# A graph attention layer: ten of 32 row tiles get one product of 258 columns in place of two

## The reference

```python
h = maximum(layernorm(x), 0.0)
h = h @ W.T + b_W
e = (h @ a1)[:, None] + (h @ a2)[None, :] + b_a[0]
e = where(e > 0, e, 0.2 * e)
scores = where(adj > 0, e, -9e15)
out = x + softmax(scores, axis=1) @ h
```

## Time and profile before

| | |
|---|---|
| Median of 3 runs | 200.91 us (200.64 to 201.04) |
| The profiled execution | 200.99 us |
| Its span in the profile | 199.4 us |
| TensorE, products | busy 194.2 us (97%), 3183 instructions |
| TensorE, weight loads | busy 188.5 us (95%) |
| VectorE | busy 184.0 us (92%) |
| ScalarE | busy 142.7 us (72%) |
| GpSimd | busy 53.0 us (27%) |
| TensorE's granted clock | full (2.4 GHz) in all slices |
| Data moved | 75.66 MB, mean 379 GB/s |

### The profile page before, as it was taken

One profiled execution on the slowest core, in us unless ns is written; L12 is line 12 of the kernel. 1 busy time (PEld: TensorE's weight loads), 2 busy tenths in 40 slices (PEclk: granted clock), 3 DMA queues, 4 the chain that ended last, 5 costly groups with the idle time before them and its releaser, 6 DMA issues.

```text
span 199.4 us, 7226 instructions
## 1 busy us (share of the span) xinstructions
PE 194.2 (97%) x3183; PEld 188.5 (95%) x3183; DVE 184.0 (92%) x269; ACT 142.7 (72%) x164; POOL 53.0 (27%) x79
## 2 busy tenths in 40 slices
PE   7989999999999999999999999999999999999993
PEld 7758889999999999999999999999999999999992
DVE  4795987899999999999999999999999999999865
ACT  2598879988886888676888888858768888888100
POOL 1028999699999020430000000000000000000000
PEclk9999999999999999999999999999999999999999
DMA  5999999999999999999999999999999999999312
GB/s 172 371 417 415 368 406 421 421 426 412 423 417 420 417 417 421 414 419 424 416 414 422 419 421 422 416 422 417 417 411 416 412 396 421 421 413 293 98 39 69
DMA packets 16256, 75.66 MB, mean 379 GB/s; under 512 B 1632, under 2 KB 5984, under 8 KB 8032
## 3 DMA queue, kind: packets, MB, share of 16 engines
q1 hardware_dynamic: 16080, 75.06, 92.6%
q10 hardware_dynamic: 144, 0.13, 0.3%
HBM read 73.08 MB, written 2.11 MB: 377 GB/s over the span
## 4 chain that ended last, share of the span: by engine, by line
PE 95%; DVE 2%; ACT 1%; issue 1%; POOL 0%; POOLq 0%
PE ps L845 28%; PE ps L841 28%; PE ps L843 28%; PE ps L817 4%; PE ps L807 3%; PE ps L898 2%; ACT L401 1%; PE ps L829 1%; DVE den L492 1%; PE ps L924 1%; PE ps L831 0%; PE ps L853 0%; DVE xT L538 0%; DVE rg L496 0%; ACT hT L337 0%
## 5 line engine op out<-in xcount | busy, mean ns | idle before, releaser
L841 PE MATMUL ps<-V,w 128*128 128x130 f16 x1008 | 170.7, 220 | 0.0
L845 PE MATMUL ps<-V,w 128*128 128x130 f16 x1008 | 170.7, 220 | 0.0
L843 PE MATMUL ps<-V,w 128*128 128x128 f16 x1008 | 170.7, 219 | 0.0
L379 ACT ACTIVATE mask<-adj_sb 128x1024 bf16<-128x1024 int32 x126 | 126.3, 1049 | 33.1 <-DMA adj_sb<-in_adj_t 32.9
L446 DVE SCALAR_TENSOR_TENSOR w<-g_row,pairs,mask 128x1024 f32<-128x1024 f32 x96 | 119.4, 1298 | 1.0 <-ACT mask L379 0.9
L843 PEld LDWEIGHTS ps<-V,w 128*128 128x128 f16 x1008 | 98.6, 98 | 1.0 <-issue 1.0
L841 PEld LDWEIGHTS ps<-V,w 128*128 128x128 f16 x1008 | 98.6, 98 | 0.7 <-issue 0.7
L845 PEld LDWEIGHTS ps<-V,w 128*128 128x128 f16 x1008 | 98.7, 98 | 0.0
L446 DVE SCALAR_TENSOR_TENSOR w<-ps,pairs,mask 128x1024 f32<-128x1024 f32 x31 | 37.5, 1274 | 3.9 <-ACT mask L379 2.7
L797 POOL PARTITION_ALL_REDUCE bad<-bad x1 | 0.4, 382 | 110.6 <-DVE bad L519 110.6
L727 POOL TENSOR_TENSOR x_sb<-x_sb,b_row 128x512 f32<-128x512 f32 x8 | 10.9, 1404 | 0.0
(11 more groups left out here) (103 smaller groups left out, 67.0 us busy)
## 6 DMA issues: line engine op xcount, KB each, us to landing
adj_sb<-in_adj_t SPq DMA_DIRECT2D x64, 1024.0 KB, 10.4
xT<-in_x_t SPq DMA_DIRECT2D x8, 256.0 KB, 7.5
x_sb<-in_x_p SPq DMA_DIRECT2D x3, 512.0 KB, 12.0
g_row<-g_dram SPq DMA_DIRECT2D x3, 512.0 KB, 11.2
out<-xT SPq DMA_DIRECT2D x3, 512.0 KB, 9.6
x_sb<-in_x_p SPq DMA_DIRECT2D x2, 256.0 KB, 4.3
out<-xT SPq DMA_DIRECT2D x1, 192.0 KB, 3.2
out<-xT SPq DMA_DIRECT2D x3, 64.0 KB, 1.6
```

Of the source, the lines that this page charges most:

```text
L379: nc.scalar.activation(mask[:, m % MASKS, r], adj_sb[:, m % HELD, r], ACT.Relu, scale=CONNECTED).then_inc(mask_ready, 1)
L841: nc.tensor.matmul(sums[:, bank, a, :], w16[:, m % SLOTS, col:col + P, 1], V[:, jt, 0, 0:NF], start=(jt == 0 and a == 0), stop=False, skip ...
L843: nc.tensor.matmul(sums[:, bank, a, 0:DOUT], w16[:, m % SLOTS, col:col + P, 1], V[:, jt, 1, 0:DOUT], start=False, stop=False, skip_group_c ...
L845: return nc.tensor.matmul(sums[:, bank, a, :], w16[:, m % SLOTS, col:col + P, 0], V[:, jt, 0, 0:NF], start=False, stop=(jt == NT - 1), ski ...
```

## The change

V's layout becomes 128 columns of low V, then 128 of high V, then the two of e^v, 258 columns without a gap. Ten row tiles are "parted": one of the eight in groups 0 and 2 (k = 6), five in group 1 (k = 0 to 4), three in group 3 (k = 0, 2, 4). For these the two products of the high weight become one of 258 columns, which leaves high weight by low V in 128 columns of PSUM and all the rest in the 130 columns after them. The product of the low weight stays as it is, and adds into the 130. In the rows, VectorE takes both halves: one instruction for the low half, later one for the high half, which waits for the first over a new semaphore (rows_begun). The sums of weights are read at other places; in groups 0 and 2 this takes three reductions in place of two. PIECES becomes 2, 2, 2, 1, 1 row tiles (before 3, 2, 1, 1, 1). Before the first pair of group 1 TensorE gets one more wait, for the weights of all of group 0.

```diff
-    VW = DOUT + 8
+    HI = DOUT
+    VW = HI + NF + 6
+    MERGED = HI + NF
...
-    PIECES = ((0, 3), (3, 5), (5, 6), (6, 7), (7, 8))
+    PIECES = ((0, 2), (2, 4), (4, 6), (6, 7), (7, 8))
...
+        if group % 2 == 0:
+            return (k // 3, k % 3 * NF) if k < 6 else (2, (k - 6) * MERGED)
         if group < NG - 1:
-            return 3 * (group % 2) + k // 3, k % 3
-        return ((3, 0), (3, 1), (3, 2), (4, 0), (4, 1), (5, 0), (6, 0), (7, 0))[k]
+            return (3 + k, 0) if k < 5 else (k - 2, MERGED)
+        return ((3, 0), (3, MERGED), (4, 0), (4, MERGED), (5, 0), (5, MERGED), (6, 0), (7, 0))[k]
+    def parted(group, k):
+        if group % 2 == 0:
+            return k == 6
+        return k < 5 if group < NG - 1 else k in (0, 2, 4)
...
-        V = sb("V", [P, NT, 2, VW], F16)
+        V = sb("V", [P, NT, VW], F16)
...
+                def add_rows(group, k0, k1):
+                    for k in range(k0, k1):
+                        g = GI * group + k
+                        if parted(group, k):
+                            ins = nc.vector.scalar_tensor_tensor(Z[:, g, :], low_sums(group, k), rg[:, g:g + 1], x_sb[:, g, :],
+                                                                 ALU.mult, ALU.add)
+                            ins.then_inc(rows_begun, 1)
+                        else:
+                            ins = nc.vector.scalar_tensor_tensor(Z[:, g, :], high_sums(group, k)[:, 0:DOUT], rg[:, g:g + 1],
+                                                                 x_sb[:, g, :], ALU.mult, ALU.add)
+                    for k in range(k0, k1):
+                        g = GI * group + k
+                        if parted(group, k):
+                            dve.wait_ge(rows_begun, apart.index(g) + 1)
+                            ins = nc.vector.scalar_tensor_tensor(Z[:, g, :], high_sums(group, k)[:, 0:DOUT], rg[:, g:g + 1],
+                                                                 Z[:, g, :], ALU.mult, ALU.add)
+                    return ins
...
-                    nc.tensor.matmul(sums[:, bank, a, :], w16[:, m % SLOTS, col:col + P, 1], V[:, jt, 0, 0:NF],
-                                     start=(jt == 0 and a == 0), stop=False, skip_group_check=True)
-                    nc.tensor.matmul(sums[:, bank, a, 0:DOUT], w16[:, m % SLOTS, col:col + P, 1], V[:, jt, 1, 0:DOUT],
-                                     start=False, stop=False, skip_group_check=True)
-                    return nc.tensor.matmul(sums[:, bank, a, :], w16[:, m % SLOTS, col:col + P, 0], V[:, jt, 0, 0:NF],
+                    first = jt == 0 and sums_at(group, k)[1] == 0
+                    if parted(group, k):
+                        nc.tensor.matmul(both_sums(group, k), w16[:, m % SLOTS, col:col + P, 1], V[:, jt, 0:MERGED],
+                                         start=first, stop=(jt == NT - 1), skip_group_check=True)
+                    else:
+                        nc.tensor.matmul(high_sums(group, k), w16[:, m % SLOTS, col:col + P, 1], V[:, jt, HI:HI + NF],
+                                         start=first, stop=False, skip_group_check=True)
+                        nc.tensor.matmul(low_sums(group, k), w16[:, m % SLOTS, col:col + P, 1], V[:, jt, 0:DOUT],
+                                         start=False, stop=False, skip_group_check=True)
+                    return nc.tensor.matmul(high_sums(group, k), w16[:, m % SLOTS, col:col + P, 0], V[:, jt, HI:HI + NF],
                                             start=False, stop=(jt == NT - 1), skip_group_check=True)
...
                     if m == PAIRS:
                         pe.wait_ge(h_ready, NCH)
+                        pe.wait_ge(w_ready, 2 * PAIRS)
```

More of the change, by code:

```diff
@@ L96, in sums_at @@
     def sums_at(group, k):
+        if group % 2 == 0:
+            return (k // 3, k % 3 * NF) if k < 6 else (2, (k - 6) * MERGED)
         if group < NG - 1:
-            return 3 * (group % 2) + k // 3, k % 3
-        return ((3, 0), (3, 1), (3, 2), (4, 0), (4, 1), (5, 0), (6, 0), (7, 0))[k]
+            return (3 + k, 0) if k < 5 else (k - 2, MERGED)
[4 more added lines that the diff above has]
+        return k < 5 if group < NG - 1 else k in (0, 2, 4)
+    apart = [GI * group + k for group in range(NG) for k in range(GI) if parted(group, k)]
     with ExitStack() as ctx:
@@ L163, in gat_layer_kernel, with high_sums, low_sums, both_sums @@
         Z = xT[:].rearrange("p (g d) -> p g d", d=DIN)
-        sums = ps[:, :, 0:3 * NF].rearrange("p b (a n) -> p b a n", a=3)
+        def high_sums(group, k):
+            bank, at = sums_at(group, k)
+            at += HI if parted(group, k) else 0
+            return ps[:, bank, at:at + NF]
+        def low_sums(group, k):
+            bank, at = sums_at(group, k)
+            return ps[:, bank, at:at + DOUT]
+        def both_sums(group, k):
+            bank, at = sums_at(group, k)
+            return ps[:, bank, at:at + MERGED]
         w16 = w[:, :, :].rearrange("p a n -> p (a n)").bitcast(F16).rearrange("p (a n h) -> p a n h", a=SLOTS, h=2)
@@ L228, in gat_layer_kernel @@
         rg_ready = sem("rg_ready")
+        rows_begun = sem("rows_begun")
         rows_added = sem("rows_added")
@@ L466, in inverse_sums @@
                 def inverse_sums(group):
-                    first, bank = GI * group, 3 * (group % 2)
+                    first = GI * group
                     dve.wait_ge(mm_done, PAIRS * (group + 1))
-                    for a, b, k0, k1 in ((bank, 2, 0, 6), (bank + 2, 1, 6, 8)):
-                        of = sums[:, a:a + b, 0:(k1 - k0) // b, DOUT:NF]
+                    if group % 2 == 0:
+                        blocks = ((ps[:, 0:2, 0:3 * NF].rearrange("p b (a n) -> p b a n", a=3)[:, :, :, DOUT:NF], 0, 6),
+                                  (ps[:, 2:3, 0:MERGED].rearrange("p b (a n) -> p b a n", a=1)[:, :, :, HI + DOUT:MERGED], 6, 7),
+                                  (ps[:, 2:3, MERGED:MERGED + NF].rearrange("p b (a n) -> p b a n", a=1)[:, :, :, DOUT:NF], 7, 8))
+                    else:
+                        blocks = ((ps[:, 3:8, 0:MERGED].rearrange("p b (a n) -> p b a n", a=1)[:, :, :, HI + DOUT:MERGED], 0, 5),
+                                  (ps[:, 3:6, MERGED:MERGED + NF].rearrange("p b (a n) -> p b a n", a=1)[:, :, :, DOUT:NF], 5, 8))
+                    for of, k0, k1 in blocks:
                         r = slice(first + k0, first + k1)
-                        ins = nc.vector.tensor_reduce(den[:, r].rearrange("p (b a) -> p b a", b=b), of, AX_X, ALU.add)
+                        ins = nc.vector.tensor_reduce(den[:, r].rearrange("p (b a) -> p b a", b=of.shape[1]), of, AX_X, ALU.add)
                     ins.then_inc(sums_added, 1)
@@ L524, in past_rows @@
                     dve.wait_ge(xb_ready, len(SETS))
[L525 to L530, removed]
+                    of = GI // len(ROWS)
+                    add_rows(group, of * part, of * (part + 1)).then_inc(rows_added, 1)
                 def rows(i):
@@ L534, in rows @@
                     dve.wait_ge(xb_ready, len(SETS))
[L535 to L540, removed]
+                    add_rows(NG - 1, *PIECES[i]).then_inc(rows_ready, 1)
                 def statistics(i, k0=0, k1=None):
```

35 lines of the change are left out of this document (17 added, 18 removed).

## The result

The changed kernel took 203.77 us (median of 5 runs, 203.09 to 205.56), the one before 201.04 in the same runs: 1.0117 times, interval 1.0069 to 1.0164. It became slower, by 2.7 us between the medians and 2.4 us by that ratio, beyond my range of 200.5 to 201.7.

A forecast was written before the change was run, and what follows sets the result against it. TensorE was taken as the bound, with VectorE setting the end. TensorE's gain goes into the wait for weights and VectorE's larger last whole piece: +0.08 us, 200.99 to 201.07 profiled, predicted 201.0, range 200.5 to 201.7.

The forecast's parts named there:

- my mark: Start of VectorE's last inverse, 196.24 us before the change, forecast at 196.32; everything after it was taken as unchanged.
- Products: On TensorE, 318 merged products at 110.0 ns each save 2.5 ns a time: 0.80 us, 0.75 before pair 61.
- Additions: On VectorE, ten more additions at 0.26 us each; group 1's five (1.30 us) swallowed by pair 51, group 2's not.
- the price of 0.38: Rival, chance 0.08: VectorE's second halves are held until everything before has ended, 0.38 us per extra addition; 201.7 us.
- Late weights: Pair 63, side 1: weights ready at 189.04, TensorE there at 188.72, so a new wait of about 0.4 us.
- VectorE back behind the masks by pair 52: Sign that the forecast is right: VectorE loses group 1's added lag and runs behind ScalarE's masks again.
- the bound of 0.2 us: A mask stream that ran earlier would help by at most some 0.2 us before group 1's extra additions hold it.
- the rival of weights in time: Chance 0.13: pair 63's weights are not late, the last inverse starts at 195.94, 0.30 us before 196.24; 200.6 us.
- The pieces: At the end, TensorE takes 2.01 us per two-tile piece, VectorE 1.50; VectorE falls behind from the third, now whole, piece.
- Nothing saved: Rival, chance 0.10: a merged product costs 112.5 ns like the two it replaces; the end comes 0.49 us later, 201.4 us.
- weight loads: Rival, chance 0.02: TensorE's weight loads are the bound, so each dropped load saves a 56 ns slot; 200.4 us.
- A hitch late in the loads: Rival, chance 0.12: an adjacency load 1.1 us late between pairs 50 and 55 delays VectorE's last run; up to 202.1 us.

The follow-up runs named there:

- 124 waits: Changed kernel plus 124 extra TensorE waits, each met long before: 201.40 us, 0.9964 times; with wide products in groups 0 and 1 alone, 200.69 us, 0.9956 times.
- 64 not in every kernel: Changed kernel plus 64 extra TensorE waits between pairs 17 and 60, each met long before: 201.17 us, 1.0028 times the kernel before.
- 142 of the same waits: Kernel before the change plus 142 extra TensorE waits, each met long before: 203.70 us, 1.0128 times.
- a short jump: TensorE's share of the fallback path left out, so its last branch jumps over one instruction: changed kernel 201.54 us, kernel before 201.03 us.
- the first profile: First profiled execution of the changed kernel, with no further edit: 203.09 us.
- the second: Profile of the changed kernel, unedited, when run again after the last experiment: median 203.67 us, 1.0102 times.
- the half loads: From pair 15 on, half of each adjacency block loaded, except pairs with a group's diagonal: changed kernel with 64 extra TensorE waits 202.71 us, kernel before 201.79 us.

## Why the prediction was wrong

The step that failed is the one with which I set my mark: "the last inverse's start, 196.24, is my mark for it; what follows that is unchanged". What follows it holds a branch whose cost hangs on the number of instructions ahead. The change takes 636 away from TensorE (two for each of 318 products), 124 past a multiple of 256; that moved the branch from 79 instructions behind the last packet to 221, and it cost 2.90 us more. That the cause is the count and the length of the jump is shown from three sides: 124 waits mend it (64 not in every kernel), 142 of the same waits bring it into the kernel before, and a short jump takes it away in the changed kernel. That the 3 us are the loading of the target is read from the packets' times, and no run shows it by itself: in all four executions with a slow branch a packet starts 0.65 to 1.01 us into the branch, and the branch ends 1.39 to 1.49 us after that packet's end; in the nine with a quick one no packet starts while it runs. The Trainium skill, "Runtime: NRT & Kernel Launch", section "Instruction fetch mechanics", has the rule that I did not weigh: code comes in 16 KiB blocks, and a taken branch whose target is outside the window of loaded pages waits until the target's page has been fetched. The packets of 16 KB and the branches agree with it.

The other steps, in their order:

- *Products:* right. 110.0 ns each, 0.75 us saved by pair 61: TensorE began it at 186.77, 1.02 sooner than before, of which 0.27 come from the earlier start.
- *The wait at pair 16:* right, no gap there.
- *Additions:* right. They took 0.34 us alone and followed each other by 0.26, also those that depend on the addition before the last, so that neither the price of 0.38 nor its rival came true:

```profile
123.93 0.61 DVE L560 SCALAR_TENSOR_TENSOR xT<-ps,rg,x_sb 128x128 f32<-128x128 f32 x2
124.45 0.61 DVE L570 SCALAR_TENSOR_TENSOR xT<-ps,rg,xT 128x128 f32<-128x128 f32 x2
...
159.58 0.31 DVE L506 TENSOR_REDUCE den<-ps 128x6 f32<-128x12 f32 x3
```

- *Three reductions:* 0.31 where two took 0.23, so 0.08 more (I had 0.07).
- *Late weights:* near in size (0.38 forecast), but not in each execution: 0.64 us early in the first profile, 0.25 late in the second, 0.54 late in that with 64 waits (188.51 + 0.06 to 189.11). The sign "VectorE back behind the masks by pair 52" failed. From pair 43 on VectorE waits for no mask in any profile with all ten wide tiles (in the first it makes 21 weights without a gap, 1.20 us each); how late it is was settled earlier, in the profile with 64 waits at 114.95, where it last waited for a mask. So the bound of 0.2 us, with which I made the rival of weights in time small, was wrong: the first profile's weights ended at 187.81, 1.23 sooner than forecast.
- *The pieces:* right, 2.01 us on TensorE, 1.50 for the third on VectorE, and no wait behind it.
- *Nothing saved, weight loads:* the 110.0 ns exclude both. *A hitch late in the loads:* the first profile has one, 1.96 us before the masks of pair 51, but these masks ran ahead and VectorE did not wait; the half loads show that such hitches do not make the high runs. The rows of VectorE and of ScalarE:

```profile
134.47 25.20 DVE L472 SCALAR_TENSOR_TENSOR w<-g_row,pairs,mask 128x1024 f32<-128x1024 f32 x21
```

```profile
152.41 2.01 ACT L405 ACTIVATE mask<-adj_sb 128x1024 bf16<-128x1024 int32 x2 [1.96 <-DMA adj_sb<-in_adj_t]
```

With the branch quick, the times come to 1.0028 (0.998 to 1.0077) with 64 waits, where it may have been slow in some runs, and 0.9964 (0.9921 to 1.0007) with 124: not to be told from no change, which was the forecast.

The traces tell more. From the start of the first product of pair 0 to the start of the flag's instruction, a stretch that leaves out the clock's rise and the branch, it takes:

| Executions | us |
|---|---|
| Four of the kernel before (as it is, 142 waits, fallback left out, half loads) | 182.03 to 182.04 |
| Four of the changed one with the weights in time (first profile, fallback left out, 124 waits, half loads) | 181.74 |
| Two of the changed one with late weights (by 0.25 and by 0.54) | 182.02 and 182.30 |
| Two with wide products in groups 0 and 1 alone | 181.56 |

So the change saves 0.30 us when the weights are in time, just what that rival had, and what the weights are late is paid on top: -0.02 and +0.26, where the forecast had +0.08 for 0.38. Groups 0 and 1 alone save 0.48, as 190 x 2.5 ns should. How often the weights are late, and so where the median lies, stays open.

## What to carry to other kernels

A kernel whose instructions change in number moves every later branch against the blocks in which code is loaded; before forecasting a change of a few tenths of a us, count the instructions ahead of a branch at the end, look at how long it took before, and keep the jump short. When an edit costs much more than it should, look behind the last instruction that the chain of waits shows: the chain ends with data, the span does not. A margin read from one profile (1.6 us of spare weights) is a value with a spread, and a gain that uses up the margin comes only in some executions. And where runs differ at their start, compare the stretch that the change works on, from one event to another: here two sets of four executions agree within 0.01 us, while their times lie 1.6 and 3.3 us apart.

## What the runs showed of the hardware

A branch on TensorE over some 430 instructions took 0.47 to 0.49 us in seven executions, where it stood 4 to 96 instructions behind the start of the last 16 KB packet, and 3.07 to 3.64 in four, where it stood 221 to 281 behind it; over one instruction it took 0.23 to 0.24 in two. How far ahead the packets are asked for I did not find. The last ones before the branch start 171 to 199 instructions past a multiple of 256, those amid full adjacency loads mostly between 238 past one and 50 past the next. At 203 past a multiple the branch was quick in two executions and slow in one.

TensorE's clock at the start spreads the runs. It was full (2.4 GHz) from 4.16 to 5.41 us on in eight profiled executions, from 6.86 and 7.07 in two (201.42 and 201.52 us), and only from 9.20 to 10.07 in three (202.54, 202.81, and 205.23 with the slow branch as well). That the kernel before has its runs near 203.3 from the same cause is likely and not shown, as none of them was profiled. The chain of waits of the changed kernel with 124 waits (202.54 us) and of the kernel before, from some 5 us on:

```profile
5.72 1.92 PE ps L851 x2
7.63 0.43 PE ps L953 x2
8.06 1.49 PE ps L851 x2
9.55 1.92 PE ps L861 x16
```

```profile
5.61 0.96 PE ps L807 x2
6.57 0.22 PE ps L907 x2
6.79 0.86 PE ps L807 x2
7.65 1.92 PE ps L817 x16
```

The same products of 512 columns take 1.92 and 1.49 us in the one and 0.96 and 0.86 in the other, so that the next stage begins 1.9 us later. The trace has the granted clock at full (2.4 GHz) from 9.20 us on in the one and from 5.15 in the other; before that it has no record, but the doubled times are those of the half level. TensorE had done the same warm-up products ahead of it in both.
